# One-hots of the last three passes: from an SBUF ramp, or from a constant PSUM bank plus a scalar

## The chip, the cores and the metric

The kernel runs on one core of a Trainium2 chip. The metric is the device time of one execution in microseconds (us); less is better.

## What is computed

A graph network of four layers on 12500 nodes of 48 features and 212500 edges, sorted by destination. Each layer adds to the nodes something made of a layer norm, a gather over the edges and a sum per destination. Cut to what matters here:

```python
h = relu(layernorm(x)); x = x + segment_sum(h[src] * edge_weight[:, None], dst)       # layer 0
h = relu(layernorm(x)); x = x + layer1(h, ...)          # gates from an MLP, a sum over src, a layer norm
h = relu(layernorm(x)); a = softmax of edge_weight1 over the edges of a destination   # layer 2
x = x + elu(segment_sum(h[src] * a[:, None], dst))
h = relu(layernorm(x)); y1 = spmm(h); y2 = spmm(y1)     # layer 3, twice the same sum
x = x + (h + y1 + y2) / 3
# spmm(v) = segment_sum(v[src] * edge_weight[:, None], dst)
```

## The kernel before

Nodes are kept as 98 blocks (`NB`) of 128 (`P`). Edges are padded to 1664 columns of 128 (`T`), four columns to a group (`G`), so 416 groups (`NG`); a loop over 52 turns (`TURNS`) holds eight groups (`GB`) written out. Since the edges are sorted by destination, the destinations of a group lie in one node block, or in a few neighbouring ones; `ranges` holds the first and last block of each group, and engines load it into registers (`load_ranges`).

There are five passes over all edges. `first_pass` makes layer 0 and the parts of later layers that need only the edges. A pass for layer 1 follows, which scatters its messages with an accumulating indirect DMA (L1071). Then `light_pass` runs three times: for layer 2 and twice for layer 3. Between passes all engines meet.

In a light pass the engines run in parallel and are tied by semaphores:

- GpSimd (POOL) gathers. For each group it waits for its four columns of indices (`s_idx`), then issues four indirect DMAs (L725), each of which fetches 128 rows of the node table from HBM into a slot of `ring`, which has room for eight groups.
- ScalarE (ACT) copies the indices of the group six ahead (`LEAD`) into `idx` (L732) as soon as VectorE is done with a group (`s_done`), then waits for the landing of its own group and multiplies each gathered row by its edge's weight (L743).
- VectorE (DVE) makes, for each pair of a group and a node block that it touches (a window), the one-hot matrices of the four columns: element (edge, column, node) is 1 where the edge's destination is that node of the block (L775). It compares a slice of `iota` (0, 1, 2, ... as uint16 in SBUF, the same on each partition) with the destinations `dstf` (one number per edge, float32 in SBUF), both broadcast to 128 x 4 x 128. Then it adds the sums of the window before, which PE left in PSUM, to the accumulator of that block (`keep`, L765).
- PE multiplies the one-hots with the weighted rows (L801), four float32 products that accumulate in one of two PSUM banks of `psum_acc`, taken in turns.

The one-hots lie in `hot`, two buffers in the room of `table`, as `ring` does; a profile row therefore says `table` for all of them. `node` holds, for node block k, the number k x 128 + p in column k on partition p. PSUM has eight banks: two for each of `psum_acc`, `psum_exp`, `psum_mlp` and `psum_comb`. The last three and the first bank of `psum_acc` serve the first two passes, too; in the light passes only `psum_acc` is used.

Of the kernel before, what the change touches and what calls it, by code (L numbers as in the profile page):

```python
# [11 lines left out]
P = 128  # L12
# [37 lines left out]
def gnn_kernel(nc, x, dst_cols, src_cols, dst_rows, src_rows, w_cols, logit_cols, logit_rows,  # L50
# [10 lines left out]
    with ExitStack() as ctx:  # L61
# [73 lines left out]
        def ps(name, shape):  # L135
            return ctx.enter_context(nc.psum_tensor(name, shape, f32))

        psum_acc = ctx.enter_context(nc.psum_tensor("psum_acc", [P, 2, 512], f32))
        psum_exp = [ps(f"psum_exp{r}", [P, 512]) for r in range(2)]
        psum_mlp = [ps(f"psum_mlp{r}", [P, 512]) for r in range(2)]  # L140
        psum_comb = [ps(f"psum_comb{r}", [P, 512]) for r in range(2)]


# [210 lines left out]
        with nc.Block() as block:  # L354
            @block.sync
            def _(sp):

                sp.wait_ge(s_zout, ZT)
                sp.dma_start(by_partition(table0, (C, C0)), embst).then_inc(s_embout, 16)
                for k in range(2):  # L360
                    sp.wait_ge(s_h0, k + 1)
                    sp.dma_start(by_partition(table0, (0, C))[:, k * NB // 2:(k + 1) * NB // 2, :],
                                 h[:, k * NB // 2:(k + 1) * NB // 2, :]).then_inc(s_table0, 16)
                sp.wait_ge(s_table0, 32)
                sp.wait_ge(s_embout, 16)

            @block.gpsimd
            def _(pool):

                nc.gpsimd.iota(int_a[:, 0:1], pattern=[[0, 1]], base=0, channel_multiplier=1).then_inc(s_consts, 1)  # L370
                nc.gpsimd.iota(int_a[:, 1:1 + NBW], pattern=[[P, NBW]], base=0, channel_multiplier=1).then_inc(s_consts, 1)
                nc.gpsimd.iota(int_a[:, 1 + NBW:2 + NBW], pattern=[[0, 1]], base=TRASH, channel_multiplier=1).then_inc(s_consts, 1)

                pool.wait_ge(s_typec, 1)
                for q in range(ZT):
                    pool.wait_ge(s_zin[q % ZR], 16 * (q // ZR + 1))
                    if q >= 2:
                        pool.wait_ge(s_zmm, q - 1)
                    nc.gpsimd.tensor_scalar(zhot[:, q % 2, :], zc[:, q % ZR, :], typec[0:NEL, 0:1], None,
                                            ALU.is_equal).then_inc(s_zhot, 1)  # L380

            @block.vector
            def _(dve):
                link = chain(dve, "s_const_chain")
                dve.wait_ge(s_consts, 6)
                nv.tensor_copy(typec[:, :], int_a[:, 0:1]).then_inc(s_typec, 1)
                dve.wait_ge(s_eamm, 1)
                link(nv.tensor_copy(node[:, :], int_a[:, 1:1 + NBW]))
                link(nv.tensor_copy(trash[:, :], int_a[:, 1 + NBW:2 + NBW]))
                link(nv.tensor_scalar(far[:, :], node[:, :], -BIG, None, ALU.mult))  # L390
                nv.tensor_copy(ea[:, GE:2 * GE], psum_mlp[0][0:NEL, 0:GE]).then_inc(s_ea, 1)
                room = tbl_flat[:, 0:NB // 2 * C].rearrange("p (b c) -> p b c", c=C)
                layernorm_relu(link, nv, s_var, s_std, 0, nodes[:, :, :], h[:, :, :], room=room, made=s_h0)

                a, b = int_a.bitcast(f32), int_b
                k12 = 2 * CUTOFF
                link(nv.tensor_scalar(a, w[:, 0:T], -1.0, None, ALU.mult))
                link(nv.tensor_tensor(a, a, w[:, 0:T], ALU.max))
                link(nv.tensor_scalar(b, a, 1.0 / k12, None, ALU.mult))
                link(nv.scalar_tensor_tensor(out=a, in0=b, scalar=-k12, in1=a, op0=ALU.mult, op1=ALU.add))  # L400
                c = cw[:, :]
                link(nv.tensor_scalar(c, a, -1.0, None, ALU.mult))
                link(nv.tensor_tensor(a, a, c, ALU.max))
                link(nv.tensor_scalar(c, a, -1.0, k12, ALU.mult, ALU.add))
                link(nv.tensor_tensor(a, a, c, ALU.min))
                nv.tensor_scalar(a, a, -PI / CUTOFF, PI / 2, ALU.mult, ALU.add).then_inc(s_sinin, 1)
                dve.wait_ge(s_sin, 1)
                link(nv.tensor_scalar(c, c, 0.5, 0.5, ALU.mult, ALU.add))
                link(nv.scalar_tensor_tensor(out=c, in0=w[:, 0:T], scalar=CUTOFF, in1=c, op0=ALU.is_lt, op1=ALU.mult))

                dve.wait_ge(s_zout, ZT)
                dve.wait_ge(s_embout, 16)
                link(nv.memset(embq[:, NB:NBW, :, :], 0.0))
                split(link, embq[:, 0:NB, :, :], embq32, scratch[:, 0:NB * GE].rearrange("p (b c) -> p b c", c=GE))

            @block.tensor
            def _(pe):
                nc.tensor.matmul(psum_mlp[0][0:NEL, 0:GE], embts[:, :], adapts[:, :], start=True, stop=True).then_inc(s_eamm, 1)
                pe.wait_ge(s_ea, 1)
                for q in range(ZT):  # L420
                    pe.wait_ge(s_zhot, q + 1)
                    if q >= 2:
                        pe.wait_ge(s_zout, q - 1)
                    for b in range(ZB):
                        last = nc.tensor.matmul(psum_exp[q % 2][:, b * 2 * GE:(b + 1) * 2 * GE],
                                                zhot[:, q % 2, b * P:(b + 1) * P], ea[:, :], start=True, stop=True)
                    last.then_inc(s_zmm, 1)

            @block.scalar
            def _(act):  # L430
                for q in range(min(ZR, ZT)):
                    act.dma_start(zc[:, q, :], type_row[0, q * ZB * P:(q + 1) * ZB * P].partition_broadcast(NEL)).then_inc(s_zin[q], 16)
                for q in range(ZT):
                    if q == ZT - 2:
                        act.wait_ge(s_sinin, 1)
                        nc.scalar.activation(cw[:, :], int_a.bitcast(f32), ACT.Sin).then_inc(s_sin, 1)
                    act.wait_ge(s_zmm, q + 1)
                    pv = psum_exp[q % 2][:, 0:ZB * 2 * GE].rearrange("p (b c) -> p b c", c=2 * GE)
                    nc.scalar.copy(embst[:, q * ZB:(q + 1) * ZB, :], pv[:, :, 0:GE])
                    nc.scalar.copy(embq32[:, q * ZB:(q + 1) * ZB, :], pv[:, :, GE:2 * GE]).then_inc(s_zout, 1)  # L440
                    if q == 5:
                        std(act, s_var, s_std, 0)
                    if q + ZR < ZT:
                        act.dma_start(zc[:, q % ZR, :], type_row[0, (q + ZR) * ZB * P:(q + ZR + 1) * ZB * P].partition_broadcast(NEL)).then_inc(s_zin[q % ZR], 16)
# [264 lines left out]
        def light_pass(order, name, src_table, cols, weights, total, before=None):  # L709
# [7 lines left out]
            with nc.Block() as block:  # L717
# [30 lines left out]
                def _(dve):  # L748
                    if before is not None:
                        before(dve)  # L750
                    nv.memset(acc_flat, 0.0).then_inc(s_clear, 1)
                    nv.memset(psum_acc[:, :, 0:CS], 0.0).then_inc(s_clear, 1)
                    dve.wait_ge(s_clear, 2)
                    dve.sem_inc(s_done, 1)
                    if order == 0:
# [4 lines left out]
                    def keep(win, s_made):  # L760
# [2 lines left out]
                        dve.wait_ge(s_kept, win)  # L763
                        dve.wait_ge(s_picked, win + 1)
                        nv.tensor_tensor(block_acc, block_acc,  # L765
                                         psum_acc[:, ds((win + 1) & 1, 1), 0:cols].rearrange("p r c -> p (r c)"), ALU.add).then_inc(s_made, 1)

                    with dve.Fori(0, TURNS) as i:
                        spans = load_ranges(dve, i)
                        for j in range(GB):  # L770
                            dve.reg_mov(room_dve, dve.snap(wn_dve))
                            with dve.Fori(*spans[j]) as k:
                                win = dve.snap(wn_dve)
                                dve.wait_ge(s_picked, dve.snap(room_dve))
                                nv.tensor_tensor(hot[:, j % 2, :, :],  # L775
                                                 iota[:, ds(k * P, P)].unsqueeze(1).to_broadcast([P, G, P]),
                                                 dstf[:, ds(i * U + j * G, G)].unsqueeze(2).to_broadcast([P, G, P]),
                                                 ALU.is_equal).then_inc(s_spread, 1)
                                keep(win, s_kept)
                                dve.reg_mov(before_dve, k)  # L780
                                dve.reg_add(wn_dve, wn_dve, 1)
                                dve.reg_add(room_dve, wn_dve, 1)
# [4 lines left out]
                def _(pe):  # L787
# [3 lines left out]
                    with pe.Fori(0, TURNS) as i:  # L791
                        spans = load_ranges(pe, i)
                        for j in range(GB):
                            pe.wait_ge(s_weighed, i * GB + (j + 1))
                            pe.sem_inc(s_seen, 1)
                            with pe.Fori(*spans[j]) as k:
# [1 line left out]
                                pe.wait_ge(s_kept, win)  # L798
                                pe.wait_ge(s_spread, win)
                                for u in range(G):  # L800
                                    last = nc.tensor.matmul(psum_acc[:, ds(win & 1, 1), 0:cols].rearrange("p r c -> p (r c)"),  # L801
                                                            hot[:, j % 2, u, :], ring[:, j * G + u, 0:cols],
                                                            start=(u == 0), stop=(u == G - 1))
                                last.then_inc(s_picked, 1)
# [465 lines left out]
```

## Time and profile before

| | |
|---|---|
| timed runs | 12131.9 us median of 3 (12123.6 to 12135.7) |
| profiled execution, its span | 14505.6 us |
| PE, PEld busy | 6101.2 us (42%), 4794.2 us (33%) |
| DVE, ACT busy | 4404.3 us (30%), 3763.8 us (26%) |
| POOL busy | 9272.0 us (64%) |
| DMA engines | 805018 packets, 671.16 MB, mean 46 GB/s |

The profiled execution is one run of the same program with the profiler on; its own time is the span from its first to its last instruction, and it is 2373.7 us longer than the timed median. Busy time is the time in which an engine has at least one instruction under way; the idle time before an instruction is put down to what ended it ("issue" where the profile shows no wait).

### The profile page before, as it was taken

Reading aid. Unit: us, or ns where it says so; the run is one execution under the profiler, and the core shown is the slowest. Engines: PE = TensorE matmul, PEld = TensorE weight load, DVE = VectorE, ACT = ScalarE, POOL = GpSimd, SP = SyncE. Lnnn points to the kernel's source line nnn. Section 1 sums busy time; section 2 is a strip of 40 time slices with the busy share of each in tenths; the row PEclk is TensorE's granted clock in tenths of the full one; section 3 lists DMA queues with packets and bytes.
Section 4 is the critical chain, followed back from the end, with each engine's and each line's share of the span. In section 5 each row is a group of like instructions: output and inputs, shape, how many; then the busy total and the mean of one; then the engine's idle time right before and its main releaser. Section 6 shows DMA issues by size and latency. Waiting matters only on the chain. (4 is left out here: it accounts for less than half of the span.)

```text
span 14505.6 us, 217117 instructions
## 1 busy us (share of the span) xinstructions
PE 6101.2 (42%) x41742; PEld 4794.2 (33%) x41743; DVE 4404.3 (30%) x18474; ACT 3763.8 (26%) x13496; POOL 9272.0 (64%) x8348
## 2 busy tenths in 40 slices
PE   4444444444555555552333333233333333333333
PEld 2222122123444444442333333233333333333333
DVE  4444444445444444443111111211111111111111
ACT  2444444443222222221111111111111111111111
POOL 5555555555888888884666666566666666666665
DMA  4333333334455555542111111111111111111111
GB/s 115 101 102 100 97 96 95 94 96 66 62 61 61 61 61 62 61 61 47 16 16 16 16 16 16 20 16 16 16 16 16 16 22 16 16 16 16 16 16 21
DMA packets 805018, 671.16 MB, mean 46 GB/s; under 512 B 417876, under 2 KB 663828, under 8 KB 802727
## 3 DMA queue, kind: packets, MB, share of 16 engines
q0 software_dynamic: 452736, 234.14, 14.8%
q1 hardware_dynamic: 349659, 430.53, 11.3%
q10 hardware_dynamic: 2588, 6.12, 0.1%
q14 instruction: 24, 0.20, 0.0%
q8 instruction: 11, 0.18, 0.0%
HBM read 562.94 MB, written 107.13 MB: 46 GB/s over the span
## 5 line engine op out<-in xcount | busy, mean ns | idle before, releaser
L725 POOL DMA_INDIRECT table<-table,idx x4992 | 4900.3, 982 | 3003.1 <-issue 1544.4
L801 PE MATMUL psum_acc<-table 128*128 128x48 f32 (+1 forms) x12288 | 2854.8, 416 | 5083.8 <-DVE acc L765 2683.5
L801 PEld LDWEIGHTS psum_acc<-table 128*128 128x128 f32 x12288 | 2697.3, 329 | 5241.3 <-issue 5241.3
L1071 POOL DMA_INDIRECT sums<-rows,idx x1664 | 2620.6, 1575 | 577.2 <-issue 435.1
L504 POOL DMA_INDIRECT rows<-table,idx x1668 | 1689.8, 1013 | 1593.6 <-ACT idx L554 1109.8
L775 DVE TENSOR_TENSOR table<-iota,dstf 128x512 f32 x1536 | 1063.9, 693 | 2852.3 <-remote 1462.0
L732 ACT CAST idx<-srow 128x4 int32 (+1 forms) x1266 | 243.2, 193 | 6337.6 <-DVEq L783 4122.5
L765 DVE TENSOR_TENSOR acc<-acc,psum_acc x1539 | 311.8, 203 | 3547.7 <-remote 2403.7
L693 PE MATMUL psum_acc<-parts,onehot 128*128 128x48 bf16 x6144 | 338.4, 215 | 1633.2 <-DVE onehot L637 1504.7
L992 PE MATMUL psum_exp<-table,onet 128*128 x6144 | 431.8, 219 | 1384.6 <-DVE onet L915 1141.0
L743 ACT ACTIVATE table<-table,w 128x48 f32<-128x48 f32 x3328 | 840.9, 323 | 12.0 <-DMA table<-table,idx 12.0
L992 PEld LDWEIGHTS psum_exp<-table,onet 128*128 128x128 bf16 x6144 | 340.5, 116 | 1519.3 <-issue 1495.9
L693 PEld LDWEIGHTS psum_acc<-parts,onehot 128*128 128x128 bf16 x6144 | 271.3, 117 | 1718.7 <-DVE onehot L637 1574.5
L966 PE MATMUL psum_mlp<-w2s,hid 49*128 49x48 f32 x3336 | 808.3, 414 | 49.7 <-DMA hid<-hid_dram 49.7
L966 PEld LDWEIGHTS psum_mlp<-w2s,hid 49*128 49x128 f32 x3336 | 741.2, 324 | 123.4 <-issue 73.5
L1038 ACT ACTIVATE gate<-psum_mlp,adapt,cw 128x48 f32<-128x48 f32 x1664 | 515.7, 391 | 25.7 <-issue 13.6
L590 ACT ACTIVATE scratch<-drow,far 128x512 f32<-128x512 uint16 x512 | 368.5, 720 | 511.7 <-DVE segmax L655 273.9
L1020 ACT CAST parts<-rest 128x196 bf16<-128x196 f32 x416 | 150.0, 361 | 1307.1 <-DVE rest L897 964.9
L946 DVE TENSOR_TENSOR idx<-srow,dmp 128x4 int32<-128x4 f32 x416 | 68.3, 164 | 1384.5 <-POOLq L1073 1318.8
L680 PE MATMUL psum_mlp<-srcrow,w1s 40*48 40x512 f32 x416 | 397.0, 1056 | 152.3 <-issue 115.6
L652 DVE TENSOR_TENSOR acc<-acc,psum_acc 128x48 f32 x512 | 104.7, 205 | 1134.1 <-remote 1075.5
L562 ACT CAST parts<-rest 128x192 bf16<-128x192 f32 x417 | 147.6, 354 | 1155.2 <-DVE rest L621 1056.2
(183 smaller groups left out, 7772.8 us busy)
## 6 DMA issues: line engine op xcount, KB each, us to landing
drow<-rows_dram SPq DMA_DIRECT2D x832, 128.0 KB
lrow<-in_logit_rows SPq DMA_DIRECT2D x416, 256.0 KB
table<-table,idx POOLq DMA_INDIRECT x4992
srcrow<-rows_dram SPq DMA_DIRECT2D x416, 128.0 KB
hid_dram<-hid SPq DMA_DIRECT2D x416, 96.0 KB
hid<-hid_dram SPq DMA_DIRECT2D x416, 96.0 KB
rows<-table,idx POOLq DMA_INDIRECT x1668
sums<-rows,idx POOLq DMA_INDIRECT x1664
```

Of the source, the lines that this page charges most:

```text
L504: pool.indirect_dma_start(out=rows[:, u, 0:width], out_offset=None, in_=src_table, in_offset=bass.IndirectOffsetOnAxis(ap=idx[:, u:u + 1], ...
L590: nc.scalar.activation(pen[:, :], drow[:, j % 2, :], ACT.Abs, scale=BIG, bias=far[:, ds(k, 1)]).then_inc(s_pen, 1)
L680: nc.tensor.matmul(psum_mlp[j % 2][0:C, :], w1s[:, :], attr[j % 2], start=True, stop=True).then_inc(s_mlp1, 1)
L693: last = nc.tensor.matmul(psum_acc[:, 0, 0:cols], onehot[:, u, :], parts[:, j % 2, u, q, 0:cols], start=(u == 0 and q == 0), stop=(u == G ...
L725: pool.indirect_dma_start(out=ring[:, u, 0:cols], out_offset=None, in_=src_table, in_offset=bass.IndirectOffsetOnAxis(ap=idx[:, u:u + 1], ...
L743: last = nc.scalar.activation(ring[:, j * G + u, 0:cols], ring[:, j * G + u, 0:cols], ACT.Copy, scale=weights[:, ds(i * U + (j * G + u), 1)])
L775: nv.tensor_tensor(hot[:, j % 2, :, :], iota[:, ds(k * P, P)].unsqueeze(1).to_broadcast([P, G, P]), dstf[:, ds(i * U + j * G, G)].unsqueez ...
L801: last = nc.tensor.matmul(psum_acc[:, ds(win & 1, 1), 0:cols].rearrange("p r c -> p (r c)"), hot[:, j % 2, u, :], ring[:, j * G + u, 0:col ...
L966: last = nc.tensor.matmul(psum_mlp[j % 2][:, u * C:(u + 1) * C], hid[:, j % 2, u * P:(u + 1) * P], w2s[:, :], start=True, stop=True)
L992: last = nc.tensor.matmul(psum_exp[j % 2][:, u * CT:(u + 1) * CT], onet[:, u * P:(u + 1) * P], table[:, ds(k, 1), q, :].rearrange("p b c - ...
L1038: last = nc.scalar.activation(gate[:, j % 2, u, 0:C], psum_mlp[j % 2][:, u * C:(u + 1) * C], ACT.Identity, scale=cw[:, ds(t, 1)], bias=ada ...
L1071: pool.indirect_dma_start(out=sums[c], out_offset=bass.IndirectOffsetOnAxis(ap=idx[:, slot:slot + 1], axis=0), in_=rows[:, slot, 0:CS], in ...
```

## The change

The two banks of `psum_acc` are parted. One stays for the first pass; the other becomes `psum_step`, a constant that is written once in the setup: `step[p, c] = c - node[p, 0]`, which is c - p. The light passes accumulate in the two banks of `psum_mlp`, which they did not use before and which now are one tensor, `psum_pair`. A one-hot is made as (step + node[:, k]) == destination: step + node[:, k] is (c - p) + (128 k + p) = 128 k + c, the number that the slice of `iota` held. The tensor_tensor with two SBUF operands becomes a scalar_tensor_tensor with one operand in PSUM, one in SBUF and a per-partition scalar in SBUF.

```diff
-        psum_acc = ctx.enter_context(nc.psum_tensor("psum_acc", [P, 2, 512], f32))
+        psum_acc = ctx.enter_context(nc.psum_tensor("psum_acc", [P, 1, 512], f32))
+        psum_step = ps("psum_step", [P, 512])
+        step = psum_step[:, 0:P]
         psum_exp = [ps(f"psum_exp{r}", [P, 512]) for r in range(2)]
-        psum_mlp = [ps(f"psum_mlp{r}", [P, 512]) for r in range(2)]
+        psum_pair = ctx.enter_context(nc.psum_tensor("psum_pair", [P, 2, 512], f32))
+        psum_mlp = [psum_pair[:, r, :] for r in range(2)]
...
                 link(nv.tensor_copy(trash[:, :], int_a[:, 1 + NBW:2 + NBW]))
+                link(nv.tensor_scalar(step, iota[:, 0:P], node[:, 0:1], None, ALU.subtract))
...
-                    nv.memset(psum_acc[:, :, 0:CS], 0.0).then_inc(s_clear, 1)
+                    nv.memset(psum_pair[:, :, 0:CS], 0.0).then_inc(s_clear, 1)
...
                         nv.tensor_tensor(block_acc, block_acc,
-                                         psum_acc[:, ds((win + 1) & 1, 1), 0:cols].rearrange("p r c -> p (r c)"), ALU.add).then_inc(s_made, 1)
+                                         psum_pair[:, ds((win + 1) & 1, 1), 0:cols].rearrange("p r c -> p (r c)"), ALU.add).then_inc(s_made, 1)
...
-                                nv.tensor_tensor(hot[:, j % 2, :, :],
-                                                 iota[:, ds(k * P, P)].unsqueeze(1).to_broadcast([P, G, P]),
-                                                 dstf[:, ds(i * U + j * G, G)].unsqueeze(2).to_broadcast([P, G, P]),
-                                                 ALU.is_equal).then_inc(s_spread, 1)
+                                nv.scalar_tensor_tensor(out=hot[:, j % 2, :, :], in0=step.unsqueeze(1).to_broadcast([P, G, P]),
+                                                        scalar=node[:, ds(k, 1)],
+                                                        in1=dstf[:, ds(i * U + j * G, G)].unsqueeze(2).to_broadcast([P, G, P]),
+                                                        op0=ALU.add, op1=ALU.is_equal).then_inc(s_spread, 1)
...
-                                    last = nc.tensor.matmul(psum_acc[:, ds(win & 1, 1), 0:cols].rearrange("p r c -> p (r c)"),
+                                    last = nc.tensor.matmul(psum_pair[:, ds(win & 1, 1), 0:cols].rearrange("p r c -> p (r c)"),
```

## Rows read from the trace of the kernel before

**Rows 1.** The page's first line.

```profile
span 14505.6 us, 217117 instructions
```

**Rows 2.** GpSimd's groups: busy us, mean ns; idle us before, who ended it.

```profile
L725 POOL DMA_INDIRECT table<-table,idx x4992 | 4900.3, 982 | 3003.1 <-issue 1544.4 <-ACT idx L732 1458.6
L1071 POOL DMA_INDIRECT sums<-rows,idx x1664 | 2620.6, 1575 | 577.2 <-issue 435.1 <-ACT rows L1026 78.1 <-DMA sums<-rows,idx 38.7
L504 POOL DMA_INDIRECT rows<-table,idx x1668 | 1689.8, 1013 | 1593.6 <-ACT idx L554 1109.8 <-issue 483.8
```

**Rows 3.** GpSimd's waits: us in total, times, longest us.

```profile
POOL table L725 <- issue: 1544.4, 4687, 3.6
POOL table L725 <- ACT idx L732: 1458.6, 305, 103.8
POOL rows L504 <- ACT idx L554: 1109.8, 221, 32.2
```

**Rows 4.** Two gather lines: min/median/max ns, first and last start.

```profile
L504 POOL DMA_INDIRECT rows<-table,idx x1668: 939/947/1491, 125.1 to 3375.3; - x186
L725 POOL DMA_INDIRECT table<-table,idx x4992: 939/947/4915, 6677.8 to 14476.5; - x200
```

**Rows 5.** Timeline, starts of the last two passes: start, us, instruction [idle <-releaser].

```profile
9312.16 0.94 POOL L725 DMA_INDIRECT table<-table,idx  x1 [72.36 <-ACT idx L732]
...
11899.46 4.92 POOL L725 DMA_INDIRECT table<-table,idx  x1 [23.25 <-ACT idx L732]
11903.59 5.06 DVE L1209 SCALAR_TENSOR_TENSOR nodes<-h,nodes 128x4704 f32<-128x4704 f32 x1
11904.68 4.79 POOL L725 DMA_INDIRECT table<-table,idx  x1 [0.30 <-issue]
```

**Rows 6.** Timeline, 9009 to 9028 us: a stall.

```profile
9022.01 0.20 DVE L765 TENSOR_TENSOR acc<-acc,psum_acc  x1 [13.38 <-remote]
...
9026.35 0.19 ACT L732 CAST idx<-srow 128x4 int32 x1 [17.76 <-DVEq L783]
...
9027.33 1.00 POOL L725 DMA_INDIRECT table<-table,idx  x1 [5.18 <-ACT idx L732]
```

**Rows 7.** Timeline, 9322 to 9331 us: ScalarE near a pass's start.

```profile
9323.65 1.01 ACT L743 ACTIVATE table<-table,w 128x48 f32<-128x48 f32 x4 [3.34 <-DMA table<-table,idx]
...
9328.72 1.01 ACT L743 ACTIVATE table<-table,w 128x48 f32<-128x48 f32 x4 [3.98 <-DMA table<-table,idx]
```

**Rows 8.** Timeline, 9000 to 9005 us: builds and gathers.

```profile
9000.43 0.69 DVE L775 TENSOR_TENSOR table<-iota,dstf 128x512 f32 x1 [0.61 <-issue]
9000.54 1.40 POOL L725 DMA_INDIRECT table<-table,idx  x1 [0.30 <-issue]
...
9003.14 0.69 DVE L775 TENSOR_TENSOR table<-iota,dstf 128x512 f32 x1 [0.62 <-issue]
9003.49 1.16 POOL L725 DMA_INDIRECT table<-table,idx  x1 [0.30 <-issue]
```

**Rows 9.** Timeline, 8048 to 8050 us: an accumulation and a gather.

```profile
8048.48 0.21 DVE L765 TENSOR_TENSOR acc<-acc,psum_acc  x1 [6.00 <-remote]
8048.61 0.94 POOL L725 DMA_INDIRECT table<-table,idx  x1 [0.30 <-issue]
```

**Rows 10.** Timeline, 168 to 170 us, in the first pass.

```profile
168.49 0.18 DVE L662 CUSTOM_DVE_ANT_0 dots<-rows,psum_exp 128x32 f32<-128x32 f32 x1
168.54 0.94 POOL L504 DMA_INDIRECT rows<-table,idx  x1 [0.30 <-issue]
```

**Rows 11.** The page's costliest groups: the builds.

```profile
L775 DVE TENSOR_TENSOR table<-iota,dstf 128x512 f32 x1536 | 1063.9, 693 | 2852.3 <-remote 1462.0
```

**Rows 12.** VectorE's groups by shape, 3300 to 6600 us.

```profile
L934 DVE SCALAR_TENSOR_TENSOR dmp<-srow,trash,dup 128x4 f32<-128x4 f32 x416 | 90.1, 217 | 0.0
L946 DVE TENSOR_TENSOR idx<-srow,dmp 128x4 int32<-128x4 f32 x416 | 68.3, 164 | 1384.5 <-POOLq L1073 1318.8 <-issue 65.4
L940 DVE TENSOR_TENSOR lg<-lg,psum_exp 128x4 f32 x408 | 61.6, 151 | 0.0
```

## The prediction

> **What bounds the kernel now.** I read the page first, then GpSimd's groups and waits, then timelines of a few microseconds inside the last three passes, where the edit is. The page puts GpSimd (POOL) far ahead of the other engines, and its three groups of indirect transfers fill the span one after the other: the gathers of the first pass, the scatters of the second and the gathers of the last three [rows 2].
>
> The profiled execution has a span of 14505.6 us [rows 1], and the timed runs a median of 12131.9 us, 2373.7 us less. So I have to say which idle time of the profile the timed runs do not have. GpSimd waits for ScalarE's indices for 1458.6 us in the last three passes and 1109.8 us in the first [rows 3]. One such wait is in [rows 6]: VectorE sits 13.38 us for something that the profile can't name ("remote"), ScalarE then waits 17.76 us for VectorE's sequencer, and GpSimd at last 5.18 us for ScalarE, though nothing in the code needs so long. Add up what GpSimd does without these waits:
>
> - before its first gather 125.1 [rows 4];
> - first pass: 1689.8 busy and 483.8 issue idle [rows 2];
> - second pass: 2620.6 busy and 577.2 idle [rows 2];
> - last three passes: 4900.3 busy and 1544.4 issue idle [rows 2];
> - the three waits that are real, at the start of each of these passes, while the passes before them drain and layer norms run: 103.8 [rows 3], 72.36 and 23.25 [rows 5];
> - after the last gather: 14505.6 - 14476.5 - 0.95 = 28.2 [rows 1, 4].
>
> The sum is 12168.9 us, 37 us or 0.3% above the timed median. The waits left out are 1109.8 - 32.2 (the longest one, which lies before the first gather and is in the 125.1) and 1458.6 - 199.4, together 2336.8, and 12168.9 + 2336.8 is the span again. So in a timed run GpSimd practically never waits for another engine inside the passes: the timed kernel is GpSimd's own chain, and a microsecond taken off a gather comes off the time. The start of a pass, before the first stall, shows the same from the other side: ScalarE waits 3.34 and 3.98 us of a group's 5.07 us (9323.65 to 9328.72) for the gathered rows to land [rows 7]. Everything behind the gathers has time to spare.
>
> **What the edited instruction does to that chain.** An undisturbed gather takes 0.94 to 0.95 us, and the next one starts 0.30 us later [rows 8, 9]. The mean of the 4992 is 982 ns [rows 2]. [Rows 8] show where the rest comes from. A one-hot build (L775, 0.69 us, two SBUF operands) starts at 9000.43; the gather that starts at 9000.54, 0.11 us into it, takes 1.40 us and ends at 9001.94, 0.82 us after the build's end. The next build starts at 9003.14; a gather 0.35 us into it takes 1.16 us and ends at 9004.65, again 0.82 us after. So the gather is held near its start until the build is over, and loses about 0.57 us less its offset into the build. At the start of the third of these passes two big operations on two SBUF operands hold a gather 4.92 and 4.79 us [rows 5]; the second (L1209) is a scalar_tensor_tensor with a constant scalar, the operation that the change brings in.
>
> With one operand in PSUM there is no hold: a gather that starts 0.13 us into an L765 (SBUF plus PSUM) takes 0.94 us [rows 9], and one that starts 0.05 us into an L662 (SBUF and PSUM, 0.18 us) takes 0.94 us too [rows 10].
>
> **The change part by part.**
>
> *The 1536 builds* become scalar_tensor_tensor with in0 = the constant bank (PSUM), in1 = the destinations (SBUF) and node[:, k] as a per-partition scalar. If they hold no gather, the loss goes. Its size in the profile: 4900.3 - 4992 x 0.945 = 182.9 us [rows 2], less 4.92 + 4.79 - 2 x 0.945 = 7.8 for the two gathers held by L1208 and L1209 [rows 5], which stay: 175 us. In the timed run it is probably more, because in the profile a share of the builds ran while GpSimd was idle: 1259.2 (1458.6 - 199.4) of 4900.3 + 1544.4 + 1259.2 = 7703.9 us, 16.3%. That gives 175 / 0.837 = 209 us. A second way: gathers start every 1.25 us, so a build that falls anywhere costs 0.57 x 0.57 / (2 x 1.25) = 0.13 us on average, times 1536 builds [rows 11] = 200 us. Bounds: the chain without the 175 is 11994 us, so if all else in the timed runs is as profiled they hold only 138 us of it. If the idle rows called issue are all 0.30 to 0.31 us in the timed runs (4687 x 0.305 = 1429.5 of the 1544.4 [rows 3]), another 115 us of the chain is not there and they hold 253. I take 209, and 138 to 253 for the range.
>
> *The build's own length.* A scalar_tensor_tensor with a per-partition scalar on 4 elements takes 217 ns where a tensor_tensor on 4 takes 164; one operand in PSUM adds nothing (151) [rows 12]. So 693 + 53 = 746 ns. Nothing at 0, and at most 1536 x 0.053 = 81 us if VectorE were the bound; I take nothing, because it lies under the 3.3 to 4.0 us that ScalarE waits for each landing [rows 7].
> A rule of the Trainium skill speaks against the change here: VectorE: DVE Perf Modes, section "The TRN2 errata", gives a PSUM source 120 cycles of fixed cost against 58 from SBUF. That would be an estimated 65 ns more per build, 811 ns in all, and the sum would be the same, since the same landing waits cover it; [rows 12] do not show it.
>
> *What the new form leaves open.* In every row of before that holds nothing, the SBUF operand comes first and PSUM second, and no scalar is read per partition. The new build has SBUF second and a scalar from SBUF. From below: it holds nothing, as the L765 and L662 rows, 209 us of gain; from above: it holds like L775 and longer, a loss (first rival). I take the first, as the nearer row by operand count.
> The Trainium skill, page SBUF — State Buffer, section "SBUF: two separate sides", has VectorE take the port pair that it shares with GpSimd when an operation has two SBUF inputs (against GpSimd operations that read SBUF), and hold it for the whole instruction. By that rule, which says nothing of their order, the sum is the one above; the trace agrees with the held half, and no row here shows SBUF second.
>
> *The setup subtraction* into the bank is one VectorE instruction of 128 columns once, some 0.3 us by the 4-element rows [rows 12] plus 124 columns at 1.35 ns (693 / 512). *The accumulator* moves to the two banks of psum_pair: same shapes, same counts, nothing reads them then. *Index arithmetic* on VectorE's sequencer loses a multiplication by 128. No transfer is moved, no wait is added, and no queue sees another order. Together at 0, at worst 1 us.
>
> **Sum.** 12131.9 - 209 = 11923 us, 1.7% less.
>
> **Rivals.**
>
> 1. *The new build holds GpSimd too* (through the second operand's port or the scalar's read) and is longer. The stretch of starts that lose grows from 0.57 to 0.57 + 0.053 us, the mean loss with its square, 1.195 times: 209 becomes 250, so 12173 us, 0.3% slower. For it: no row has this operand order, and L1209 shows that the operation holds with two SBUF operands. Against: the hold disappears in both rows with one PSUM operand, of two operations. It decides at the first gather that starts inside a build and takes over 1.0 us. Chance 0.12.
> 2. *Holds as before and the length doesn't matter*: the phase of the builds against the gathers shifts so that the longer stretch costs under 0.2%. 12132 us, chance 0.08.
> 3. *The gathers get shorter and GpSimd waits for ScalarE instead.* The profile's stalls would have to be in the timed runs too; GpSimd's lead of six groups would then eat the 209. Against: with the 1259 us the chain would be 13428, far above 12131.9. 12132 us, chance 0.06.
>
> The forecast has 0.74. Its own range is 11870 to 12000 (138 and 253 of gain, and some 8 us for the rest). About a tenth of its chance lies outside that, so to hold 8 in 10 the range must reach up to the second and third rivals: 11860 to 12145. A change under 0.2% (24 us; the three runs spread over 12) can't be told from none. Faster 0.75, same 0.12, slower 0.13.
>
> **What would show it.** Right: L775 reads SCALAR_TENSOR_TENSOR of about 0.75 us; the mean gather in the last passes falls from 982 to some 947 ns and GpSimd's busy time there from 4900 to about 4725 us; gathers that start inside a build take 0.95 us; only the two beside L1208 and L1209 stay long. The profiled span should fall by less than the timed one, since part of the gain there goes into the waits for ScalarE. Wrong: gathers of 1.1 to 1.5 us still follow the builds (rivals 1 and 2), or short gathers with the timed median unmoved (rival 3), or a build over 3 us: it would use up the 3.34 us that ScalarE waits per group [rows 7], with 1536 / 1248 builds to a group, and put VectorE in the way.

## The result and the profile after

| | timed median, us | runs |
|---|---|---|
| before | 12132.35 | 12123.6 to 12135.7 (4) |
| changed | 11978.14 | 11976.67 to 11987.37 (4) |

The ratio is 0.9876, 95% interval [0.9862, 0.989]: 154 us faster, where 209 were forecast (11923 us).

The first profile of the kernel before carried long stalls that neither the timed runs nor the profile of the changed kernel have, so a new profile of the kernel before (the control run below, span 12136.4 us) stands beside the one after (11985.6 us); their spans differ by 150.8 us. For the same reason the forecast's sign that the profiled span should fall by less than the timed one can't be read: from the first profile to the one after it falls by 2520.0 us.

GpSimd's groups, first of the changed kernel (L729 was L725, L1075 was L1071, L508 was L504; rows of before: [rows 2]). After the bar: busy us and mean ns, then idle us before them and what ended it.

```profile
L729 POOL DMA_INDIRECT table<-table,idx x4992 | 4718.0, 945 | 1699.4 <-issue 1509.3 <-ACT idx L736 190.1
L1075 POOL DMA_INDIRECT sums<-rows,idx x1664 | 2620.8, 1575 | 576.5 <-issue 429.3 <-ACT rows L1030 73.0 <-DMA sums<-rows,idx 44.4
L508 POOL DMA_INDIRECT rows<-table,idx x1668 | 1717.5, 1030 | 542.6 <-issue 475.3 <-ACT idx L558 67.3
```

The same of the control run:

```profile
L725 POOL DMA_INDIRECT table<-table,idx x4992 | 4868.4, 975 | 1699.7 <-issue 1510.0 <-ACT idx L732 189.7
L1071 POOL DMA_INDIRECT sums<-rows,idx x1664 | 2620.3, 1575 | 576.7 <-issue 424.8 <-ACT rows L1026 72.1 <-DMA sums<-rows,idx 51.2
L504 POOL DMA_INDIRECT rows<-table,idx x1668 | 1717.2, 1029 | 543.2 <-issue 475.9 <-ACT idx L554 67.3
```

Five of the six numbers that matter are the same to within a microsecond: two passes' busy and idle times, and the idle time of the gathers that the change touches. One differs: the 4992 gathers of the last passes are busy 150.4 us less, and the span is 150.8 us shorter. Nothing of it was given back.

The builds, from VectorE's groups by line from 5400 us to the end of the changed kernel (before: [rows 11]):

```profile
L779 DVE SCALAR_TENSOR_TENSOR table<-psum_step,node,dstf 128x512 f32<-128x512 f32 x1536 | 1153.0, 751 | 2287.2 <-PE psum_pair L805 1438.7 <-issue 848.6
```

A build is 58 ns longer and still has idle time in front of it. And a build with a gather in it, from the timeline of the changed kernel (before: [rows 8]):

```profile
5709.91 0.75 DVE L779 SCALAR_TENSOR_TENSOR table<-psum_step,node,dstf 128x512 f32<-128x512 f32 x1 [0.54 <-issue]
5710.05 0.94 POOL L729 DMA_INDIRECT table<-table,idx  x1 [0.30 <-issue]
```

The gather starts 0.14 us into the build and takes 0.94 us. At nearly that offset, 0.11 us, [rows 8] have 1.40 us. In the whole trace a gather starts inside 757 of the 1536 builds, and none of these gathers takes over 0.97 us.

### The profile page after: what moved, and what is told of

Read it like the earlier page. It is cut to its first block and busy times, and to the rows that moved or that the text cites. A ratio compares the mean times of both kernels' runs of the same rounds, so it can differ in the third digit from the quotient of the medians.

```text
span 11985.6 us, 215771 instructions
## 1 busy us (share of the span) xinstructions
PE 6174.3 (52%) x41742; PEld 4825.2 (40%) x41743; DVE 4528.4 (38%) x18475; ACT 3744.7 (31%) x13496; POOL 9117.1 (76%) x8348
## 5 line engine op out<-in xcount | busy, mean ns | idle before, releaser
L729 POOL DMA_INDIRECT table<-table,idx x4992 | 4718.0, 945 | 1699.4 <-issue 1509.3
L805 PE MATMUL psum_pair<-table 128*128 128x48 f32 (+1 forms) x12288 | 2934.0, 417 | 3508.8 <-ACT table L747 2848.4
L805 PEld LDWEIGHTS psum_pair<-table 128*128 128x128 f32 x12288 | 2728.9, 328 | 3713.9 <-issue 3709.8
L1075 POOL DMA_INDIRECT sums<-rows,idx x1664 | 2620.8, 1575 | 576.5 <-issue 429.3
L508 POOL DMA_INDIRECT rows<-table,idx x1668 | 1717.5, 1030 | 542.6 <-issue 475.3
L779 DVE SCALAR_TENSOR_TENSOR table<-psum_step,node,dstf 128x512 f32<-128x512 f32 x1536 | 1153.0, 751 | 2287.2 <-PE psum_pair L805 1438.7
L769 DVE TENSOR_TENSOR acc<-acc,psum_pair x1539 | 311.3, 202 | 2517.7 <-PE psum_pair L805 2497.6
L970 PE MATMUL psum_pair<-w2s,hid 49*128 49x48 f32 x3336 | 808.3, 414 | 53.1 <-DMA hid<-hid_dram 53.1
L970 PEld LDWEIGHTS psum_pair<-w2s,hid 49*128 49x128 f32 x3336 | 741.2, 324 | 126.8 <-issue 72.3
L747 ACT ACTIVATE table<-table,lg 128x49 f32<-128x49 f32 x1664 | 421.9, 324 | 1098.8 <-DMA table<-table,idx 1094.2
L572 ACT ACTIVATE prod<-rows,w 128x48 f32<-128x48 f32 x1668 | 421.0, 323 | 460.9 <-DMA rows<-table,idx 459.8
L1042 ACT ACTIVATE gate<-psum_pair,adapt,cw 128x48 f32<-128x48 f32 x1664 | 515.7, 391 | 25.8 <-issue 13.7
L684 PE MATMUL psum_pair<-srcrow,w1s 40*48 40x512 f32 x416 | 396.9, 1056 | 147.6 <-issue 101.8
```

The costliest lines, as they stand in the source:

```text
L508: pool.indirect_dma_start(out=rows[:, u, 0:width], out_offset=None, in_=src_table, in_offset=bass.IndirectOffsetOnAxis(ap=idx[:, u:u + 1], ...
L572: last = nc.scalar.activation(prod[:, j % 2, u, 0:cols], rows[:, j % RING * G + u, 0:cols], ACT.Copy, scale=weights[:, ds(i * U + (j * G + ...
L684: nc.tensor.matmul(psum_mlp[j % 2][0:C, :], w1s[:, :], attr[j % 2], start=True, stop=True).then_inc(s_mlp1, 1)
L729: pool.indirect_dma_start(out=ring[:, u, 0:cols], out_offset=None, in_=src_table, in_offset=bass.IndirectOffsetOnAxis(ap=idx[:, u:u + 1], ...
L747: last = nc.scalar.activation(ring[:, j * G + u, 0:cols], ring[:, j * G + u, 0:cols], ACT.Copy, scale=weights[:, ds(i * U + (j * G + u), 1)])
L779: nv.scalar_tensor_tensor(out=hot[:, j % 2, :, :], in0=step.unsqueeze(1).to_broadcast([P, G, P]), scalar=node[:, ds(k, 1)], in1=dstf[:, ds ...
```

## Experiments

### The kernel before again, and where the operand lies

**Control.** The kernel before without an edit.

> The kernel before once more, for a profile like the one of the changed kernel (11985.6 us, without the long stalls). Theory: the whole gain of 154 us is hold taken off the gathers of the last three passes, so here their mean is 945 + 154000/4992 = 976 ns plus the 8 us beside L1208 and L1209 (2 ns), 978 ns in all; issue idle as in the changed kernel, about 1509 us, and the waits for ScalarE's indices about 190 to 200 us. Rival: the builds hold 209 us as predicted (mean 987 to 989 ns) and something in the changed kernel took 55 us back. Span about 12130 us by both.

Measured: 12138.1 us (one run), mean gather 975 ns (group above). The waits for ScalarE, 189.7 us, are little but the three real ones at the passes' starts, and in the first pass 67.3 us are left of [rows 3]'s 1109.8. The builds hold 150 us, not 209, and the changed kernel gains just that. The theory stands and the rival falls. (Its 2 ns for the gathers beside L1208 and L1209 were counted twice: the changed kernel's 945 ns hold them already.)

**Ramp in SBUF.** The changed kernel, with one edit:

```diff
-        step = psum_step[:, 0:P]
+        step = sb("step_sb", [P, P])[:, :]
```

> The changed kernel with the constant ramp in SBUF instead of PSUM: the same scalar_tensor_tensor, the same scalar, the same accumulator banks, but two SBUF operands. Theory: the hold is back and grows with the length (about 0.75 us against 0.69), so the gathers' mean is near 978 to 988 ns and the time 12120 to 12200 us, like before or up to 0.5% slower. Rival: the gain came from the new operation or the moved accumulator, not from where the operand lies; then the time stays at 11978 us and the gathers at 945 ns.

Measured: 12130.4 us (10 runs), ratio to before 0.9996 [0.9987, 1.0006]. The gathers are back at 974 ns; from the groups of this kernel:

```profile
L729 POOL DMA_INDIRECT table<-table,idx x4992 | 4863.8, 974 | 1698.4 <-issue 1509.0 <-ACT idx L736 189.4
L779 DVE SCALAR_TENSOR_TENSOR table<-step_sb,node,dstf 128x512 f32<-128x512 f32 x1536 | 1154.4, 752 | 2330.6 <-PE psum_pair L805 1483.4 <-issue 847.2
```

So the whole gain is where the ramp lies; the new operation, its scalar and the moved accumulator give nothing. Two more things can be read here. The PSUM operand makes a build no longer (751 ns against 752). And the longer build does not cost more: 752 ns builds hold the gathers 4863.8 - 4718.0 = 146 us, 693 ns builds 150 us. The part of the theory that let the loss grow with the length is wrong, because the stretch of starts that lose does not grow: gathers of over 975 ns start 0.046 to 0.534 us into a build of the control run, and 0.097 to 0.600 us into one of this run, 0.49 and 0.50 us long.

**Operands swapped.** `in0` = destinations, `in1` = ramp, `op0=ALU.subtract`.

> The changed kernel with the operands in the other order: (destination - node) == ramp, SBUF first and the PSUM ramp second. Theory: the hold depends on how many SBUF operands there are and not on their order, so 11978 us within 12 us and a mean gather of 945 ns. Rival: the place matters (the changed kernel is free only because its SBUF operand stands second); then gathers of 1.1 to 1.5 us return and the time is near 12130 us.

Measured: 11977.79 us (one run), gathers 4717.4 us busy, 945 ns. The number of SBUF operands decides, not their order.

### When the build runs

The loss per build was 150 / 1536 = 0.098 us, under the 0.13 that the prediction gave for a build at a random moment. These runs move the builds of the kernel before by memsets of PSUM banks that the last passes don't use:

```diff
                                 dve.wait_ge(s_picked, dve.snap(room_dve))
+                                dve.wait_ge(s_shift, win)
+                                nv.memset(psum_comb[0][:, 0:430], 0.0)
+                                nv.memset(psum_comb[1][:, 0:430], 0.0).then_inc(s_shift, 1)
                                 nv.tensor_tensor(hot[:, j % 2, :, :],
```

The first run has one memset of 260 columns, the second two of 280, the third the two above; the fourth is the changed kernel with the two above.

> The kernel before with one memset of an unused PSUM bank (260 columns, some 0.3 to 0.35 us with its wait) ahead of each one-hot build of the last three passes. Memsets hold no gather, so only the moment of the build moves. Theory (the builds stand in a fixed phase to the gathers, because they follow the landing of a group, and the hold depends on that phase): moved on every gather start of the changed kernel by this much, the builds would cost 70 to 100 us in place of the measured 147, so 12055 to 12085 us. Rival (a build falls anywhere in the 1.25 us between gather starts): the loss stays at 147 us whatever the shift, 12115 to 12145 us.

> The same with two memsets of 280 columns, some 0.65 to 0.7 us. Theory of the fixed phase: a loss of 150 to 170 us, 12130 to 12155 us, above the shift of 0.35 us by some 70 us. Rival (anywhere): 12115 to 12145 us, like each of the shifts.

> The same with two memsets of 430 columns, some 0.95 to 1.05 us. Theory of the fixed phase: the worst of the shifts, a loss of 230 to 290 us, 12215 to 12275 us. Rival (anywhere): 12115 to 12145 us. If VectorE were the bound, 1536 x 1.0 us would be added: 13600 us.

> The changed kernel with the same two memsets of 430 columns ahead of each build. Its builds hold nothing, so their phase can't matter, and VectorE has 2287 us of idle time there: 11978 us within 15 us by every theory but one, in which the extra VectorE time itself costs (up to 1536 x 1.0 us).

In the last two runs the build waits for the memset (`dve.wait_ge(s_shift, win + 1)` between the two, the wait before the memset left out), with one memset of 330 columns and with the two of 430:

> The kernel before with one memset of 330 columns ahead of each build and the same wait between them, so that only the moment of the build moves, by some 0.45 us. Fixed phase (worked out from the gather starts of the changed kernel, where nothing is held): a loss of 70 to 110 us against 147, 12050 to 12090 us. Anywhere in the cycle: 147 to 196 us, 12115 to 12175 us. The shift of 0.3 us gave 171 us, so I no longer expect the first.

> The shift of two memsets of 430 columns once more, with one wait added: the build is not sent before the second memset has ended. In the run without that wait gathers were held from some 0.4 us before the build's start, that is from the second memset's start. Theory A (a build holds gathers already while it stands behind another operation of VectorE): with the wait the hold begins with the build, the loss falls from some 577 us to at most 290, the mean gather from 1062 to at most 1003 ns and the time from 12558 to at most 12280 us. Theory B (the loss of 577 us is the phase alone): the wait moves the build by less than 0.1 us, and the time stays above 12450 us.

Measured, with the gathers' busy time in the last passes less the 4718.0 us of the changed kernel as the hold (each ratio and difference is to the runs of before beside it, medians of 12125.2 and 12126.0 us):

| run | time, us | ratio to before, 95% | against before, us | hold, us |
|---|---|---|---|---|
| before (hold of the control run) | 12125.2, 12126.0 | | 0 | 150 |
| 260 | 12152.97 | 1.0024 [1.0012, 1.0035] | +28 | 175 |
| 280 + 280 | 12354.33 | 1.0187 [1.0157, 1.0217] | +229 | 376 |
| 430 + 430 | 12557.95 | 1.0355 [1.0325, 1.0385] | +433 | 581 |
| 330, build waits | 12350.02 | 1.0185 [1.0164, 1.0205] | +224 | 369 |
| 430 + 430, build waits | 12223.08 | 1.008 [1.006, 1.01] | +97 | 245 |
| changed, 430 + 430 | 11982.42 | 0.988 [0.9852, 0.9909] | -143 | 0 |

In each row the time moves with the hold within 7 us (a hold of 581 is 431 above 150, the time is 433 above). The memsets themselves cost next to nothing: in the last row VectorE does 0.83 us more for each window, 1281 us in all, and the ratio to before is 0.988 where the changed kernel has 0.9876.

Now the moment. With one memset of 260 columns a build starts 0.18 us after the memset's start (the median; the memset takes 0.275 us, and the two overlap). With one of 330 columns and the wait it starts 0.333 us and 394.4 / 1536 = 0.257 us of idle time after it, 0.59 in all and more than the 0.45 expected. The builds' length stays (675 and 695 ns), and the hold goes from 150 to 175 and 369 us. From the groups of the second of these runs:

```profile
L779 DVE TENSOR_TENSOR table<-iota,dstf 128x512 f32 x1536 | 1067.9, 695 | 394.4 <-DVE psum_comb L777 394.4
L777 DVE MEMSET psum_comb<- 128x330 f32 x1536 | 511.5, 333 | 2196.0 <-PE psum_acc L805 1440.2 <-issue 755.8
```

Counted in the traces, builds inside which a gather of over 975 ns starts are 515 of 1536 in the control run, 511 with 260 columns and 900 with 330. Such gathers start in some 0.49 us of a build (0.046 to 0.534 us in the control run), so a random moment would give 0.49 / 1.25 = 39%, 600 builds, in each. The run with 330 columns is far from that, so the phase of the builds against the gathers decides, as the theory had it, and "anywhere in the cycle" is out. But my numbers from it were wrong in size and even in sign (70 to 100 and 70 to 110 us): I had worked them out from the gather starts of the changed kernel, where no hold moves later gathers. How the phase settles stays open.

The table has a second finding: the same two memsets cost 581 us without a wait and 245 with one, as theory A of that run had it (at most 290). The timeline without the wait shows where the hold begins:

```profile
5689.00 0.42 DVE L779 MEMSET psum_comb<- 128x430 f32 x1
5689.16 1.65 POOL L726 DMA_INDIRECT table<-table,idx  x1 [0.30 <-issue]
5689.33 0.67 DVE L780 TENSOR_TENSOR table<-iota,dstf 128x512 f32 x1
```

The gather starts 0.17 us before the build, inside the memset, and is held all the same: 1.65 us, to 5690.81, which is 0.81 us after the build's end at 5690.00. In the changed kernel with the same memsets, at nearly the same place:

```profile
5855.30 0.42 DVE L783 MEMSET psum_comb<- 128x430 f32 x1
5855.39 0.94 POOL L730 DMA_INDIRECT table<-table,idx  x1 [0.30 <-issue]
5855.62 0.67 DVE L784 SCALAR_TENSOR_TENSOR table<-psum_step,node,dstf 128x512 f32<-128x512 f32 x1
```

It isn't the memset that holds. And in the kernel before with the wait between:

```profile
5656.40 0.42 DVE L778 MEMSET psum_comb<- 128x430 f32 x1
5656.87 0.94 POOL L726 DMA_INDIRECT table<-table,idx  x1 [0.30 <-issue]
5657.08 0.69 DVE L780 TENSOR_TENSOR table<-iota,dstf 128x512 f32 x1 [0.26 <-DVE psum_comb L778]
```

A gather 0.21 us before the build goes free. That is so in the whole traces: without the wait 416 gathers that start before their build, by up to 0.38 us, are held, and this is 299 us of the hold; with the wait none is. The rest of the difference is the moment, since the wait also moves the builds by 0.35 us: gathers that start inside a build cost 275 us without it and 238 with it. With two memsets of 280 columns 396 gathers are held that start up to 0.25 us before their build, 259 us of the 376.

With one memset and no wait it is not so. From the run with 260 columns:

```profile
6588.85 0.28 DVE L778 MEMSET psum_comb<- 128x260 f32 x1 [0.54 <-issue]
...
6589.02 0.95 POOL L726 DMA_INDIRECT table<-table,idx  x1 [0.30 <-issue]
6589.04 0.70 DVE L779 TENSOR_TENSOR table<-iota,dstf 128x512 f32 x1
```

Of 112 gathers in that trace that start between the memset's start and the build's, none takes over 0.96 us. So in these runs a build that is sent behind two memsets holds gathers before it starts, from about the end of the first memset (within 0.06 us, in both lengths); behind one memset, or kept back by a wait, it does not. What makes the difference between one and two stays open.

### The first pass too

**One-hots of the first pass** (L641) from the PSUM ramp:

```diff
-                                nv.tensor_tensor(onehot[:, :, :], iota[:, ds(k * P, P)].unsqueeze(1).to_broadcast([P, G, P]),
+                                nv.scalar_tensor_tensor(out=onehot[:, :, :], in0=step.unsqueeze(1).to_broadcast([P, G, P]),
+                                                        scalar=node[:, ds(k, 1)],
...
```

> The changed kernel with the one-hots of the first pass made the same way (L641, 512 builds of bf16 one-hots). In the changed kernel the 1668 gathers of that pass take 1030 ns on average, 142 us over 945 ns, and GpSimd waits there for ScalarE only 67 us. Theory: GpSimd's chain is the bound there too; L641 gives a part of the 142 us and two other kinds of operation (L646, L651) keep theirs: 30 to 90 us less, 11890 to 11950 us. Rival: VectorE is the bound of the first pass, and a build 0.06 us longer costs 512 x 0.06 = 31 us: 11980 to 12010 us.

Measured: 11944.17 us, ratio to before 0.9845 [0.9828, 0.9861], 34 us under the changed kernel (the two profiled spans differ by 42 us). The gathers of that pass fall from 1717.5 to 1650.3 us busy (989 ns), 67 us; the scatters of the second pass took 19 of it back (2624.9 busy and 591.4 idle, against 2620.8 and 576.5). Why they do was not tried.

**And the masked logits in PSUM:**

```diff
-        pen = scratch[:, 0:GW]
+        pen = psum_comb[0][:, 0:GW]
```

> The changed kernel with the first pass's one-hots from the PSUM ramp (11944 us by itself) and its masked logits, which ScalarE writes for the maximum, in an unused PSUM bank in place of SBUF: the tensor_tensor_reduce L652 then has one SBUF operand. Gathers of that pass that started inside an L652 took 1214 ns on average, 227 of them: 61 us of hold. Theory: most of it goes, 11885 to 11915 us, and the mean gather of that pass falls from 989 to some 952 ns. Rival: VectorE or ScalarE becomes the bound of that pass, 11940 us or more.

Measured: 11881.31 us, ratio to before 0.9799 [0.9783, 0.9816], the fastest of all: 245 us under the runs of before beside it (12126.0), where the changed kernel was 154 under its own. GpSimd's groups in it:

```profile
L730 POOL DMA_INDIRECT table<-table,idx x4992 | 4717.3, 945 | 1699.5 <-issue 1509.4 <-ACT idx L737 190.1
L1076 POOL DMA_INDIRECT sums<-rows,idx x1664 | 2625.1, 1578 | 587.4 <-issue 422.4 <-ACT rows L1031 84.6 <-DMA sums<-rows,idx 57.5
L508 POOL DMA_INDIRECT rows<-table,idx x1668 | 1588.4, 952 | 548.1 <-issue 471.9 <-ACT idx L558 76.2
```

The first pass's gathers come down to 952 ns, as expected. The tensor_tensor_reduce that reads the logits has one SBUF operand now. GpSimd's waits for ScalarE in that pass, 76.2 us, are 11 above those of the run before (65.3), and neither ScalarE nor VectorE became the bound.

## Why the prediction was right, and where its size was off

- *GpSimd's chain is the timed kernel.* Right. The sum of 12168.9 us rested on leaving out 2336.8 us of waits; the control run has them gone (1109.8 + 1458.6 us of waits for ScalarE have become 67.3 + 189.7), and in eight runs the time followed the gathers' busy time within 7 us. The third rival, that the saved time would turn into waits for ScalarE, is out: 189.7 before, 190.1 after.
- *A build with two SBUF operands holds a gather that starts in it; one PSUM operand does not.* Right, for either order and with the per-partition scalar, which the rows of before could not show; so the first two rivals are out. The ramp put back in SBUF brings the whole loss back. But for the PSUM half the rows that the prediction named are no evidence. By its own reading a held gather ends 0.82 us after the operation's end, so one that starts 0.13 us into the 0.21 us of an L765 [rows 9] would take 0.90 us if it were held, and one 0.05 us into the 0.18 us of an L662 [rows 10] 0.95 us: no longer than an undisturbed one. These operations are too short to show a hold, so that this half came out right was in part luck. The changed kernel's builds show it: none of the gathers that start in 757 of them is held. The Trainium skill, page SBUF — State Buffer, section "SBUF: two separate sides", counts the SBUF inputs too, and the trace agrees (975 and 974 ns with two, 945 with one).
- *The build's own length.* 746 ns forecast, 751 measured, and free, as said. The Trainium skill's rule on the 120 cycles of a PSUM source (VectorE: DVE Perf Modes, section "The TRN2 errata") does not show: 751 ns from PSUM, 752 from SBUF.
- *The size.* 209 us forecast, 154 measured. The step that failed is the term of the hold, which measures 150 us. The 175 us in the first profile were scaled up by 1 / 0.837 for the time in which GpSimd stood idle there, as if the builds in the timed runs fell on gathers as often as those did outside that time. They do not: 850 of the first profile's 1536 builds have a gather of over 975 ns start inside them, 515 of the control run's. The second way took a random moment and let every start in the first 0.57 us of a build lose. In the control run a gather that starts in the first 0.04 us goes free, which leaves 0.52 x 0.52 / (2 x 1.25) = 0.108 us a build, 166 us in all. So the agreement of the two ways, 209 and 200, was luck and no check. The lower bound of 138, from the timed median itself, was the better estimate, also with luck: beside the control run its terms for the first pass are 55 us too low, and those for the last passes' issue idle and waits and for the time after the last gather 54 us too high.
- *The first rival's price* rested on the stretch of starts that lose growing with the length. It does not: 0.50 us for 752 ns builds, which held 146 us, 0.49 us for 693 ns builds, which held 150. Had that rival come true, the time would have been that of before, 12130 us, and not 12173.

## What to carry to other kernels

Where GpSimd's indirect transfers are the chain that sets the time, look at what VectorE runs with two SBUF operands: moving one operand to PSUM, even at a longer operation, gave back all of the hold, and each such operation in any pass is worth the same look (three edits here: 245 us of 12126). Price the hold from a profile as long as the timed run, and by the holds that are counted there, not by a random moment: the same operation cost 150 to 369 us depending on when it ran. And a change of VectorE's order ahead of such an operation is not free even where VectorE is idle half the time.

## What the runs showed of the hardware that I had not expected

- An operation with two SBUF operands can hold indirect transfers before it starts: with two memsets of 0.42 us ahead, gathers up to 0.38 us before the build's start were held until after its end (1.65 us for one 0.17 us ahead), and a wait in front of the build took that away (581 us of hold down to 245, with the builds also 0.35 us later). Behind one memset of 0.28 us no gather was held before the build.
- The hold works the other way for a moment only: where a gather starts within about 0.03 us of a build's start (19 builds of 1536 in the control run), it goes free and the build is longer, but by 65 ns at most (its median of 692 ns against its maximum of 757, below), not by the gather's 945. Line L775 of the control run, with minimum, median and maximum ns:

```profile
L775 DVE TENSOR_TENSOR table<-iota,dstf x1536: 691/692/757, 5661.1 to 12114.4; 128x512 f32 x192
```

  With the ramp in PSUM both stay apart; the changed kernel's builds lie between 749 and 753 ns:

```profile
L779 DVE SCALAR_TENSOR_TENSOR table<-psum_step,node,dstf x1536: 749/751/753, 5660.6 to 11963.6; 128x512 f32<-128x512 f32 x192
```
